# Routed feed-forward network: the hidden product in PSUM, the scatter of the rows moved into the routed stage, table values read between loads

## What is computed

```python
def _L0_ffn_ref(hidden_states, gate_w, w_gate, w_up, w_down):
    B, S, D, FF, E = (4, 512, 512, 2048, 2)
    x = hidden_states.reshape(-1, d)
    logits = x @ gate_w.T
    probs = softmax(logits)
    sel = jnp.argmax(probs, axis=-1)
    top_w = take_along_axis(probs, sel[:, None], axis=-1)
    onehot = one_hot(sel, gate_w.shape[0])
    g = jnp.einsum('td,efd->etf', x, w_gate)
    u = jnp.einsum('td,efd->etf', x, w_up)
    h = jax.nn.silu(g) * u
    y = jnp.einsum('etf,edf->etd', h, w_down)
    out = jnp.einsum('etd,te->td', y, onehot * top_w)
...
xn = _layernorm(x, axis=-1)
s = _L0_attn_ref(xn, ...)
g = _silu(_L0_ffn_ref(xn, ...))
x = x + s * g
...
```

## Time and profile before

| what | value |
|---|---|
| median of 3 runs | 2151.9 us (2150.13 to 2156.42) |
| the profiled execution | 2152.38 us |
| its span, first to last instruction | 2150.6 us |
| mean granted TensorE clock | 0.919 |
| PE busy, share of the span | 1805.1 us, 84% |
| DVE busy | 1303.9 us, 61% |
| POOL busy | 1050.0 us, 49% |
| ACT busy | 851.9 us, 40% |
| dispatch stage, first to last scatter landed | about 44 to 93 us |
| routed stage | about 95 to 734 us |

### The profile page before, as it was taken

One profiled execution on the slowest core, in us unless ns is written; L12 is line 12 of the kernel. 1 busy time (PEld: TensorE's weight loads), 2 busy tenths in 40 slices (PEclk: granted clock), 3 DMA queues, 4 the chain that ended last, 5 costly groups with the idle time before them and its releaser, 6 DMA issues. The chain is left out here.

```text
span 2150.6 us, 29625 instructions
## 1 busy us (share of the span) xinstructions
PE 1805.1 (84%) x10016; PEld 1476.0 (69%) x10016; DVE 1303.9 (61%) x1913; ACT 851.9 (40%) x1426; POOL 1050.0 (49%) x658
## 2 busy tenths in 40 slices
PE   3289999999999698986749957765999999997996
PEld 2178998989899533433337846654899999995775
DVE  5156556565555569999725622662666666665886
ACT  3043333333333145556322211442666666661211
POOL 0445344443534234645413366111777787764554
PEclk7689999999999899998869977887999999998998
DMA  5353233232323501222481032102688878885664
GB/s 205 145 174 118 89 117 102 90 130 88 104 101 108 202 20 35 83 69 83 160 325 46 20 116 95 50 0 91 237 281 282 284 277 281 285 260 192 210 203 135
DMA packets 106858, 316.86 MB, mean 147 GB/s; under 512 B 14531, under 2 KB 16161, under 8 KB 105505
## 3 DMA queue, kind: packets, MB, share of 16 engines
q1 hardware_dynamic: 89536, 266.07, 36.2%
q0 software_dynamic: 17248, 49.86, 6.9%
HBM read 248.17 MB, written 67.71 MB: 147 GB/s over the span
## 5 line engine op out<-in xcount | busy, mean ns | idle before, releaser
L678 DVE TENSOR_TENSOR rffn_y<-rffn_ps_y,rffn_y 128x512 f32<-128x512 f32 x272 | 176.1, 680 | 2.6 <-PE rffn_ps_y L744 1.1
L688 DVE TENSOR_TENSOR rffn_h<-rffn_ps_hidden,rffn_silu 128x256 f32<-128x256 f32 x144 | 58.7, 408 | 186.4 <-ACT rffn_silu L649 184.8
L614 POOL TENSOR_TENSOR rffn_w0l<-rffn_raw,rffn_w0h 128x1536 fp32r<-128x1536 f32 x16 | 56.1, 3504 | 201.0 <-ACT rffn_w0h L633 201.0
L723 PE MATMUL rffn_ps_hidden<-rffn_xsh,rffn_w0h 128*128 128x256 f32 x512 | 147.2, 288 | 5.6 <-POOL rffn_w0l L614 5.6
L723 PE MATMUL rffn_ps_hidden<-rffn_xsl,rffn_w0h 128*128 128x256 f32 x512 | 145.8, 285 | 0.0
L723 PE MATMUL rffn_ps_hidden<-rffn_xsh,rffn_w0l 128*128 128x256 f32 x512 | 145.8, 285 | 0.0
L649 ACT ACTIVATE rffn_silu<-rffn_ps_hidden 128x256 f32<-128x256 f32 x144 | 53.4, 371 | 231.0 <-PE rffn_ps_hidden L723 228.0
L1849 POOL DMA_INDIRECT moe_x_in<-xn_rows,moe_idx_now x94 | 97.6, 1038 | 21.2 <-issue 14.7
L723 PEld LDWEIGHTS rffn_ps_hidden<-rffn_xsh,rffn_w0h 128*128 128x128 f32 x512 | 98.7, 193 | 9.6 <-issue 6.2
L1855 POOL TENSOR_TENSOR moe_w_0l<-moe_raw,moe_w_0h 128x1536 fp32r<-128x1536 f32 x24 | 84.3, 3512 | 38.2 <-ACT moe_w_0h L1880 38.2
L723 PEld LDWEIGHTS rffn_ps_hidden<-rffn_xsl,rffn_w0h 128*128 128x128 f32 x512 | 98.9, 193 | 1.9
(11 more groups left out here) (702 smaller groups left out, 6416.5 us busy)
## 6 DMA issues: line engine op xcount, KB each, us to landing
rffn_raw<-in_ffn_w SPq DMA_DIRECT2D x80, 768.0 KB, 4.3
moe_raw<-in_moe_w SPq DMA_DIRECT2D x47, 769.5 KB, 4.4
moe_raw<-in_moe_w SPq DMA_DIRECT2D x47, 768.0 KB, 4.9
ys<-moe_y SPq DMA_DIRECT2D x47, 512.0 KB, 3.0
xs<-route_zero SPq DMA_DIRECT2D x17, 256.0 KB
rffn_x_in<-xs SPq DMA_DIRECT2D x17, 256.0 KB, 4.0
ys<-rffn_y SPq DMA_DIRECT2D x17, 256.0 KB, 2.1
y<-in_x SPq DMA_DIRECT2D x4, 1024.0 KB, 8.9
```

Of the source, the lines that this page charges most:

```text
L614: nc.gpsimd.tensor_tensor(w[b][LO][:], raw[m % 2][:], f32(w[b][HI][:]), ALU.subtract).then_inc(s_w, 1)
L678: nc.vector.tensor_tensor(y[:, 2 * u + tt, :], yb[n % 2][tt][:], y[:, 2 * u + tt, :], ALU.add)\
L688: nc.vector.tensor_tensor(h32[n % 2][:, cols], up, sil[n % 2][:, cols], ALU.mult).then_inc(s_h32, 1)
L723: last = nc.tensor.matmul(hb[n % 2][:, half, :], wu[p][:, col:col + P], xs[q][:, c, u * PR:(u + 1) * PR], start=(c == 0 and m == 0), stop= ...
```

## The change

Three things are done.

1. `h32` moves from SBUF into one PSUM bank (`hp`, both buffers in it). L688 writes PSUM, ACT's cast and L695 read PSUM. For the bank two others are given up: of the two x banks one is left (`turned`), which serves the entering tiles from number 4 on; the first four tiles use the `yb` banks. The single tile's product goes to a tile of its own in SBUF. The order in a step changes: ACT does the hidden cast ahead of the entering tiles, DVE does the low subtraction ahead of them, and PE and DVE put the down products and the adds between the first and second entering tile.
2. The 16 scatters move from the dispatch stage to the head of POOL's list in the routed stage. The tile `y` of the norm stage lives on as the routed stage's `y`, so that the source is still there. ACT and DVE (in place of POOL) split the first three weight blocks; the memset of `y` is gone, and the first group's adds become copies. SP issues weight loads 0 to 2, waits for all scatters, and then loads rows.
3. SP reads table values one by one where they are first needed, and the rest between the third weight load and the wait for the scatters.

```diff
@@ dispatch_stage
-            pool.wait_ge(s_fill, 16 * RT)
-            pool.wait_ge(s_pos, 1)
-            for t in range(NT):
-                nc.gpsimd.indirect_dma_start(
-                    out=xs_dram, out_offset=bass.IndirectOffsetOnAxis(ap=keep.pos[:, t:t + 1], axis=0),
-                    in_=y[:, t, :], in_offset=None).then_inc(s_out, 16)
-            pool.wait_ge(s_out, 16 * NT)
@@ routed_ffn_stage
-        y = a.sb("y", [P, RT, D])
+        y = keep.rows
-        h32 = [a.sb(f"h32_{i}", [P, PR]) for i in range(2)]
+        single = a.sb("h32_single", [P, P])
-        xb = [a.ps(f"x{i}", [P, KC, P]) for i in range(2)]
-        turned = xb[0]
+        hp = a.ps("h32", [P, 2, PR])
+        turned = a.ps("x", [P, KC, P])
+        enter_banks = [yb[t // 2][t % 2][:].rearrange("p (c r) -> p c r", c=KC) for t in range(4)]
+        def bank_of(t):
+
+            return enter_banks[t] if t < 2 * LEAD else turned[:]
@@ sync
             sp.dma_start(ident[:], ident_dram).then_inc(s_id, 16)
-            load_x(0)
-            load_x(1)
             load_w(0)
-            load_x(2)
-            load_x(3)
             load_w(1)
+            load_w(2)
+            for b in range(RB):
+                expert_at(b)
+                if b < RB - 1:
+                    row_at(b)
+            sp.wait_ge(s_scat, 16 * NT)
+            for t in range(4):
+                load_x(t)
+            load_w(3)
             for t in range(4, 8):
                 load_x(t)
-            for f in range(2, RB):
-                load_w(f)
+            load_w(4)
@@ gpsimd
-            nc.gpsimd.memset(y[:], 0.0).then_inc(s_zero, 1)
-            for m in range(RB - 2):
-                fill(0, m)
+            for t in range(NT):
+                nc.gpsimd.indirect_dma_start(
+                    out=xs_dram, out_offset=bass.IndirectOffsetOnAxis(ap=keep.pos[:, t:t + 1], axis=0),
+                    in_=y[:, t, :], in_offset=None).then_inc(s_scat, 16)
+            pool.wait_ge(s_w, RB - 2)
@@ scalar
+            for m in range(RB - 2):
+                fill(0, m, True)
             for t in range(2 * LEAD):
                 x_high(t)
-            for m in range(RB - 2):
-                fill(0, m, True)
...
-                    for t in entering:
-                        x_high(t)
...
-                    src = h32[n % 2][:] if u < RP else turned[:, 0, :]
+                    src = hp[:, n % 2, :] if u < RP else turned[:, 0, :]
                     nc.scalar.copy(hT[n % 2][HI][:, cols], src).then_inc(s_hhi, 1)
+                    for t in entering:
+                        x_high(t)
@@ vector
+            for m in range(RB - 2):
+                dve.wait_ge(s_whi, m + 1)
+                nc.vector.tensor_tensor(w[m][LO][:], raw[m % 2][:], f32(w[m][HI][:]), ALU.subtract).then_inc(s_w, 1)
...
-                    if not isinstance(k, int) or k >= 2:
-                        dve.wait_ge(s_h, k - 1)
...
+                        if not start:
+                            dve.wait_ge(s_hhi, k)
+                        nc.vector.tensor_tensor(hp[:, n % 2, :], hb[n % 2][:, 1, :], sil[n % 2][:], ALU.mult)\
+                          .then_inc(s_h32, 1)
+                        dve.wait_ge(s_hhi, k + 1)
+                        nc.vector.tensor_tensor(hT[n % 2][LO][:], hp[:, n % 2, :], f32(hT[n % 2][HI][:]), ALU.subtract)\
+                          .then_inc(s_h, 1)
+                        if entering:
+                            x_low(entering[0])
+                        if not start:
+                            add(k0, n - 1, (u - 1) % RU, fresh)
+                        if len(entering) > 1:
+                            x_low(entering[1])
@@ tensor
-                if t >= 2:
-                    pe.wait_ge(s_x, t - 1)
+                if t > 2 * LEAD:
+                    pe.wait_ge(s_x, t)
...
-                    for t in entering:
-                        turn_x(t)
+                    if entering:
+                        turn_x(entering[0])
                     if not start:
                         down(k - 1, k0, n - 1, (u - 1) % RU)
+                    if len(entering) > 1:
+                        turn_x(entering[1])
```

More of the change, by code:

```diff
@@ L565, in _, with row_at, expert_at @@
         def _(sp):
-            expert = [sp.value_load(keep.table[0:1, b:b + 1], min_val=0, max_val=1) for b in range(RB - 1)]
-            row = [sp.value_load(keep.table[0:1, RB - 1 + b:RB + b], min_val=0, max_val=PR * (RP - RBLOCKS[b]))
-                   for b in range(RB - 1)]
-            expert.append(sp.value_load(keep.table[0:1, 2 * RB - 2:2 * RB - 1], min_val=0, max_val=1))
+            expert, row = {}, {}
+            def row_at(b):
+                if b not in row:
+                    row[b] = sp.value_load(keep.table[0:1, RB - 1 + b:RB + b], min_val=0,
+                                           max_val=PR * (RP - RBLOCKS[b]))
+                return row[b]
+            def expert_at(b):
+                if b not in expert:
+                    at = b if b < RB - 1 else 2 * RB - 2
+                    expert[b] = sp.value_load(keep.table[0:1, at:at + 1], min_val=0, max_val=1)
+                return expert[b]
             def rows_of(dram, t):
@@ L668, in x_low, with add @@
                 cols = slice(t * P, (t + 1) * P)
-                nc.vector.tensor_tensor(xs[LO][:, :, cols], xb[t % 2][:], f32(xs[HI][:, :, cols]),
+                nc.vector.tensor_tensor(xs[LO][:, :, cols], bank_of(t), f32(xs[HI][:, :, cols]),
                                         ALU.subtract).then_inc(s_x, 1)
+            for m in range(RB - 2):
+                dve.wait_ge(s_whi, m + 1)
+                nc.vector.tensor_tensor(w[m][LO][:], raw[m % 2][:], f32(w[m][HI][:]), ALU.subtract).then_inc(s_w, 1)
             for t in range(2 * LEAD):
                 x_low(t)
-            dve.wait_ge(s_zero, 1)
-            def add(k0, n, u):
+            def add(k0, n, u, fresh=False):
                 for tt in range(2 if u < RP else 1):
                     dve.wait_ge(s_y, k0 + halves(n) + tt + 1)
-                    nc.vector.tensor_tensor(y[:, 2 * u + tt, :], yb[n % 2][tt][:], y[:, 2 * u + tt, :], ALU.add)\
-                      .then_inc(s_yadd, 1)
+                    if fresh:
+                        nc.vector.tensor_copy(y[:, 2 * u + tt, :], yb[n % 2][tt][:]).then_inc(s_yadd, 1)
+                    else:
+                        nc.vector.tensor_tensor(y[:, 2 * u + tt, :], yb[n % 2][tt][:], y[:, 2 * u + tt, :], ALU.add)\
+                          .then_inc(s_yadd, 1)
             def body(i, first, last):
@@ L684, in step @@
                     dve.wait_ge(s_sil, k + 1)
-                    if not isinstance(k, int) or k >= 2:
-                        dve.wait_ge(s_h, k - 1)
-                    up = hb[n % 2][:, 1, :] if u < RP else hb[n % 2][:, 0, P:GU]
-                    nc.vector.tensor_tensor(h32[n % 2][:, cols], up, sil[n % 2][:, cols], ALU.mult).then_inc(s_h32, 1)
-                    for t in entering:
-                        x_low(t)
-                    if u == RP:
-                        add(k0, n - 1, u - 1)
-                    dve.wait_ge(s_hhi, k + 1)
-                    src = h32[n % 2][:] if u < RP else turned[:, 0, :]
-                    nc.vector.tensor_tensor(hT[n % 2][LO][:, cols], src, f32(hT[n % 2][HI][:, cols]), ALU.subtract)\
-                      .then_inc(s_h, 1)
-                    if u < RP and not start:
-                        add(k0, n - 1, (u - 1) % RU)
+                    fresh = first and n <= RU
+                    if u < RP:
+                        if not start:
[11 more added lines that the diff above has]
+                            x_low(entering[1])
+                    else:
+                        nc.vector.tensor_tensor(single[:], hb[n % 2][:, 0, P:GU], sil[n % 2][:, cols], ALU.mult)\
+                          .then_inc(s_h32, 1)
+                        add(k0, n - 1, u - 1, fresh)
+                        dve.wait_ge(s_hhi, k + 1)
+                        nc.vector.tensor_tensor(hT[n % 2][LO][:, cols], turned[:, 0, :], f32(hT[n % 2][HI][:, cols]),
+                                                ALU.subtract).then_inc(s_h, 1)
                 walk(i, first, step)
@@ L759, in step @@
                         hidden_single(n)
-                    for t in entering:
-                        turn_x(t)
+                    if entering:
+                        turn_x(entering[0])
                     if not start:
                         down(k - 1, k0, n - 1, (u - 1) % RU)
+                    if len(entering) > 1:
+                        turn_x(entering[1])
                     if u == RP:
                         pe.wait_ge(s_h32, k + 1)
-                        nc.tensor.transpose(turned[:, 0, :], h32[n % 2][:, 0:P], ident[:]).then_inc(s_T, 1)
+                        nc.tensor.transpose(turned[:, 0, :], single[:], ident[:]).then_inc(s_T, 1)
                 walk(i, first, step)
```

25 lines of the change are left out of this document (12 added, 13 removed).

## The result

| | before | after |
|---|---|---|
| median (range) | 2152.34 us (2150.13 to 2156.42) | 2121.93 us (2120.50 to 2125.65) |
| profiled execution, span | 2152.38, 2150.6 us | 2123.35, 2121.6 us |
| first hidden sums | 116.22 us | 104.13 us |
| the second group's first hidden sums | 161.54 us | 156.03 us |
| last add of the routed stage begins | 730.80 us | 703.12 us |

The changed kernel takes 0.9855 of the time before (95% interval 0.9838 to 0.9872): 30.4 us less by the medians, 29.0 by the profiled executions. Of these, 27.7 us are won by the last add of the routed stage. Its first group begins 12.1 us sooner and is then 6.6 us longer, and the loop from the second group on is 22.2 us shorter (569.26 to 547.09 us). The last 1.3 us lie behind that add, in stages whose code is the same.

A forecast was written before the change was run, and what follows sets the result against it. PE was taken to bound the routed stage, so only its waits and late start counted. Terms 10.3 + 1.5 - 6.3 = 5.5 us before the second group plus 18.3 after it gave 23.8: 2151.9 to 2128 us, range 2120 to 2142.

The forecast's parts named there:

- Forecast A: The forecast itself: 23.8 us won, 2128 us, alone spanning 2122 to 2138; chance 0.64.
- the stall's two delays: Routed loop, once per group: silu late behind ACT's cast, low subtraction stretched to 2.57 us; PE waits 1.41 us.
- Part 1: Routed loop: product in PSUM makes every low subtraction 0.42 us; 18.3 of 19.2 us of PE waits go.
- Part 2: Scatters beside the first weight loads: three VectorE subtractions stretch them by 3.7 us (0 to 5.3), landing at 99.1.
- Rival D: Scatters: descriptors aren't held up by the subtractions; another 3.7 us won, 2124 us; chance 0.08.
- Part 3: Way in: first hidden sums start at 105.9 instead of 116.2, +10.3 us, plus 1.5 us from the clock.
- The 1.5 us from the clock: First hidden block, now directly behind turns, loses less to the half clock: gain 1.5 us (0 to 2.4).
- Part 4: First group: one bank makes second turns wait 1.0 us; 52.1 against 45.3 us, 0.5 shaved for overlap: -6.3 us.
- One sign against: First group: a clock row reading less than 1.00 under it would show the prediction wrong.
- rival E: First group: PE falls to half clock; seven such steps lose 12 us, 2164 us; chance 0.04.
- B: Routed loop: the stalls stay and only 5.5 us are won, 2146 us; chance 0.08.
- C: Way in: it wins nothing and 18.3 us are left, 2134 us; chance 0.16.

The follow-up runs named there:

- pool_writes_long: Kernel before, with POOL's weight split reading only 16 columns and writing 2400 + 1520 columns of zeros, so POOL stays busy as long; 2135.88 us.
- fills_later: Kernel before, with weight blocks 3 and 4 filled at steps 1 and 2 of a group instead of 0 and 1; 2132.77 us, 0.9894.
- no_subs: Changed kernel, with VectorE writing zeros in place of the first three weight subtractions; 2120.52 us.
- reads_first: Changed kernel, with all nine table values read ahead of the first loads; 2121.42 us.
- free_banks: Changed kernel, with the second entering tile of each first-group step in the y bank free in that step; 2114.63 us, 0.9814.
- pool_writes: Kernel before, with POOL subtracting only 16 of 1536 columns of a weight block's low part and writing zeros in the rest; 2128.82 us.
- pool_splits: free_banks with the first two weight subtractions on POOL behind the scatters, the third in step 0, and weight loads reordered; 2119.62 us, 0.9821.

## Why the prediction was right, and where its terms were off

The prediction was 2128 us with a range of 2120 to 2142; measured were 2121.93. Forecast A is what happened, with 23.8 us predicted and 30.4 measured. Point by point:

- **What bounds the kernel, and the stall's two delays**: right. pool_writes_long takes away the hold, fills_later the late silu and 1 us of the hold, and each makes the loop 22 us shorter.
- **Part 1, 18.3 us**: the mechanism right, the term too small; measured 22.2. The failing step is that the waits were priced at the sum that the view of waits gives. In the earlier trace rows PE's wait stands as 1.41 us, but from the last hidden matmul (323.25) to the down product (324.94) it is 1.69 us where a good step has 0.12 (303.97 to 304.09), and the next product comes 0.32 us later (325.26) where a good step has 0.23 (304.32). That is 1.57 + 0.09 = 1.66 us for a wait of 1.41. The lines of before that stand around those of the earlier trace rows:

```profile
303.97 0.28 PE L723 MATMUL rffn_ps_hidden<-rffn_xsh,rffn_w2l 128*128 128x256 f32 x1
...
304.32 0.40 PE L744 MATMUL rffn_ps_y<-rffn_w1l,rffn_hT1h 128*128 128x512 f32 x1
```
```profile
323.25 0.28 PE L723 MATMUL rffn_ps_hidden<-rffn_xsh,rffn_w0l 128*128 128x256 f32 x1
...
325.26 0.40 PE L744 MATMUL rffn_ps_y<-rffn_w0l,rffn_hT0h 128*128 128x512 f32 x1
```

  Over 15 waits (22.2 - 18.3) / 15 = 0.26 us each, and 1.66 - 1.41 = 0.25 is what the one wait shows. Of this 0.16 is how the view counts: from the end of the last matmul, 0.28 us behind its start, where the next would have started 0.12 behind it. The price of an instruction into PSUM was right: 432 ns for 424. So was that of PSUM as a source, 425 ns for 426; the 0.06 us that the Trainium skill ("VectorE: DVE Perf Modes", the TRN2 errata) would add don't show.
- **Part 2, stretch 3.7 us**: the mechanism right, which no_subs shows by its absence, the size too large; measured 2.1. All four meetings of the earlier trace rows and here have one pattern: an issue that begins within a subtraction ends 0.82 to 0.84 us after the subtraction's end (80.73 + 1.81 = 82.54, the subtraction at 79.94 + 1.76 = 81.70; in the earlier trace rows 1634.21 and 1633.39). In the earlier trace rows the issue began 0.38 us into the subtraction and so lost 1.23; here the three began 0.79, 0.80 and 1.20 us into it and lost 0.84, 0.83 and 0.43. The issue at 79.45, under way when the subtraction began, took 0.97 as usual. So the price depends on where in the subtraction the next issue falls, and one row can't give it. The other traces bear this out: in all fourteen, 120 issues begin within a 128x1536 subtraction, and 115 of them end 0.82 to 0.86 us after it (the longest before the first group takes 2.48 us, in reads_first, begun 0.13 us into a subtraction). The other five, begun in its first 0.04 us, take 0.95 to 0.99. Rival D, no hold at all, has fallen. The Trainium skill ("SBUF — State Buffer", Who interferes with whom) infers that a tensor_tensor does not hold up descriptor writing. The issues here were held, but each also reads its index column from SBUF, and no run separates the two, so the inference is neither borne out nor refuted; what failed is to take from it that the scatters would run free.
- **Part 3**: the first sums were predicted for 105.9 and came at 104.13: 0.5 us from the stage's start (72.88 for 73.4), 1.6 from the stretch, less 0.3 from the first row load to the sums (6.93 for 6.6). The 1.5 us from the clock were wrong in sign. The first hidden block did gain 0.7 (4.63 for 5.3), but the second lost 1.2 (4.03 for 2.87), behind a wait of 2.21 us. free_banks has no such wait and runs its second step at 1.00, but so does no_subs with the wait, so the wait isn't shown to be the cause. The windows of the two blocks:

```profile
104.13:108.76 4.63, 4.63 (x27) 4.63 (x25) 1.38 (x2) 1.98 (x3) 0.00 (x0) 0.59 0.98 375
112.31:116.34 4.03, 4.03 (x26) 4.03 (x25) 0.69 (x1) 1.96 (x2) 1.54 (x1) 0.70 0.27 69
```

- **Part 4, six waits**: right in kind, and near in size. Five of 0.82 to 0.83 us for the 1.0 predicted, steps of 6.15 for 6.3, the last three 4.78, 4.26 and 2.85 for 4.8, 4.3 and 2.8. The first step took 8.18 us for 8.7. The group is 51.9 us for the 52.1 added up, so the shave of 0.5 for overlap, taken from that, was not there.
- **The sum before the second group**: predicted 5.5, measured 161.54 - 156.03 = 5.5. That is luck in part: the first sums were 1.8 us better, clock and group 1.8 worse (51.9 for 52.1 - 0.5 - 1.5 = 50.1).
- **The whole**: 27.7 us by the last add for 23.8 predicted, all of the difference from part 1's term; the rest, 1.3 us by the profiled executions and 2.7 by the medians, is within what the unchanged stages vary by.
- **The signs that were to show it right or wrong**: the low subtraction's longest 426 ns, only the last wait of the down product, three long scatters, first sums near 106, 0.8 us of idle before every second turn: all there. One sign against stood there too, a clock below 1.00 under the first group (0.71 and 0.83). It is rival E's mechanism; it cost 1.2 us at the second hidden block, far from the five cold steps from which E decides.

Rivals B and C have fallen: the loop lost its stalls, and the way in won 5.5 us. What wasn't priced at all is that the entering tiles could have kept a second bank: those 9.4 us were to be had beside the change.

What stays open: why the granted clock comes up in step 0 in one kernel and in step 1 in another (0.71 and 0.83 in after, 0.89 and 1.00 in no_subs, 0.98 and 0.78 in reads_first, with nearly the same work). That the kernels from before with a changed fill have other groups than the 45.32 us of before lies for a good part in the wait for tile 8's rows: 1.26 us in before, 1.75 in fills_later and 1.74 in pool_writes_long (47.41 and 47.28, the third and fourth step at a granted clock of 0.85 to 0.90), none in pool_writes (43.76).

## What to carry to other kernels

When PE waits for a short VectorE instruction that is sometimes long, look at what the longest ones lie beside and count its SBUF inputs: with a POOL instruction that reads SBUF over it, a second SBUF input is held to that instruction's end. There are then three cures (one input in PSUM, POOL writing without reading, or another place in time), and the cheapest is to ask which of the two late things can be moved in time: here two lines of schedule won what the move to PSUM won, and kept the bank. A wait on PE costs more than the view of waits says, so price a stall from start to start against a good step, and after each gain in a queue's head ask what is queued behind it: the 2 to 3 us won at pool_splits' scatters were lost again as 6 us in a step whose rows were queued behind a weight load that had to wait for its buffer.

## What the runs showed of the hardware that was not expected

- A wait of PE costs about 0.26 us beyond the idle time that the view puts down to it (15 waits, 22.2 us for 18.3); in the one looked at closely 0.16 of it is the overlap of matmuls that the view doesn't count.
- The issue of an indirect DMA on POOL is held by a VectorE subtraction with both inputs in SBUF: 1.40 to 1.81 us for 0.97, up to 2.48 in reads_first, ending 0.82 to 0.86 us after the subtraction, which stays at 1.76; with VectorE writing zeros instead, 0.97. Where POOL's computing began first it is the other way round: POOL's subtraction takes its usual 3.5 us, and VectorE's 0.42 becomes 2.57, ending 0.28 us behind POOL's.
- POOL's writes of 2.10 us over VectorE's two-input subtraction do nothing (412 to 428 ns).
